# Sixteen-head attention on one core: q and k projected once per sequence and masked per quad of heads, the values' product between the two score passes of a turn

## The reference, cut to what matters

```
q = (src @ Wq + bq).reshape(B, T, 16, 8)      # k and v likewise
scores = einsum("bqhd,bkhd->bhqk", q, k) * 8 ** -0.5
probs  = softmax(scores, axis=-1)
out    = einsum("bhqk,bkhd->bqhd", probs, v).reshape(B, T, 128)
return out @ Wo + bo
```

## Time and profile before

| | us |
|---|---|
| median of 3 runs | 2275.07 (2269.94 to 2275.17) |
| profiled execution, span | 2277.2 |
| attention16, from its first matmul (163.7) to the next stage (504) | about 340 |
| busy in 163.7 to 504: PE, DVE, ACT | 332.69, 235.62, 195.37 |
| first scores (m = 0) at 169.03: 8 records at a granted clock of 0.50 | 2.08 |
| scores of m = 5, the first with turned scores, at | 180.7 |
| opening: GpSimd's last memset (L128) ends, next stage's first DVE instruction | 10.06, 13.40 |

### The profile page before, as it was taken

The page is one execution under the profiler, slowest core; times in us unless marked ns, Lnnn a source line. Parts: engine busy times, 40 slices in busy tenths (PEclk is TensorE's granted clock), DMA queues, the critical chain, the costliest instruction groups (busy, mean ns, idle before and its releaser), DMA issues. The chain is left out here.

```text
span 2277.2 us, 47255 instructions
## 1 busy us (share of the span) xinstructions
PE 2059.6 (90%) x18551; PEld 1392.9 (61%) x18551; DVE 1348.3 (59%) x3481; ACT 1049.2 (46%) x2520; POOL 631.5 (28%) x720
## 2 busy tenths in 40 slices
PE   4989999988879999698867897959999999999998
PEld 2546666657766677454555555655666666666565
DVE  2017777754555555456536884147877777677677
ACT  4235656642244454322234436345666666666222
POOL 3016930002210000103762015652333333333000
PEclk9989999998999999899986558988999999999999
DMA  2026030002110000241251013330000000000000
GB/s 62 19 29 29 2 39 2 2 5 65 18 55 1 1 1 1 69 140 22 39 138 39 2 28 114 48 87 25 1 1 1 1 1 1 1 1 1 6 15 19
DMA packets 118330, 64.44 MB, mean 28 GB/s; under 512 B 65848, under 2 KB 113248, under 8 KB 116960
## 3 DMA queue, kind: packets, MB, share of 16 engines
q1 hardware_dynamic: 106128, 52.37, 9.8%
q0 software_dynamic: 11264, 8.66, 2.7%
q10 hardware_dynamic: 720, 0.40, 0.1%
HBM read 37.54 MB, written 23.86 MB: 27 GB/s over the span
## 5 line engine op out<-in xcount | busy, mean ns | idle before, releaser
L3078 ACT ACTIVATE l_prob<-l_ps,l_neg_max 128x128 f32<-128x128 f32 (+1 forms) x512 | 208.6, 420 | 47.3 <-DVE l_neg_max L3177 42.5
L1658 ACT ACTIVATE l0a_prob<-l0a_pst 128x1024 f32<-128x1024 f32 x128 | 131.2, 1025 | 119.7 <-PE l0a_pst L1576 119.7
L2963 POOL TENSOR_TENSOR l_prob<-l_prob,l_total 128x256 f32<-128x256 f32 x128 | 78.6, 614 | 366.0 <-DVE l_total L3185 366.0
L1709 DVE TENSOR_REDUCE l0a_peak<-l0a_ps 128x4 f32<-128x1024 f32 x128 | 156.2, 1221 | 15.8 <-PE l0a_ps L1571 13.7
L1571 PE MATMUL l0a_ps<-l0a_k,l0a_q 32*128 32x256 f32 x1024 | 146.3, 405 | 3.3 <-ACT l0a_prob L1658 2.5
L680 ACT ACTIVATE l0e_hidden<-l0e_ph,l0f_b 128x512 f32<-128x512 f32 x128 | 87.9, 687 | 129.2 <-PE l0e_ph L591 129.2
L1576 PE MATMUL l0a_pst<-l0a_q,l0a_k 32*128 32x256 f32 x1024 | 145.8, 400 | 0.2 <-ACT l0a_prob L1658 0.2
L3173 DVE TENSOR_TENSOR l_ps<-l_ps,future 128x512 f32<-128x512 f32 x128 | 89.4, 699 | 93.2 <-PE l_ps L3009 93.0
L601 PEld LDWEIGHTS l0e_py<-l0f_w,l0e_hidden 128*128 128x128 f32 x1024 | 119.7, 192 | 35.0 <-ACT l0e_hidden L680 32.6
L2964 POOL TENSOR_TENSOR l_prob<-l_prob,l_total 128x512 f32<-128x512 f32 x128 | 133.2, 1041 | 0.0
L601 PE MATMUL l0e_py<-l0f_w,l0e_hidden 128*128 128x128 f32 x1024 | 129.8, 280 | 0.3 <-ACT l0e_hidden L680 0.3
(11 more groups left out here) (533 smaller groups left out, 4936.4 us busy)
## 6 DMA issues: line engine op xcount, KB each, us to landing
l_band<-zero SPq DMA_DIRECT2D x16, 272.0 KB, 7.3
x_tok<-in_x_dram SPq DMA_DIRECT2D x2, 2048.0 KB, 8.3
l2f_w<-in_L_ffn_w_dram SPq DMA_DIRECT2D x2, 2048.0 KB, 10.0
l_rows<-l_band SPq DMA_DIRECT2D x16, 256.0 KB
l1f_w<-in_L_ffn_W_dram SPq DMA_DIRECT2D x3, 1024.0 KB, 11.3
gd_tri<-gp_tri SPq DMA_DIRECT2D x8, 256.0 KB, 2.0
l0f_w<-gd_tri SPq DMA_DIRECT2D x8, 256.0 KB, 11.5
gd_tri<-l0f_w SPq DMA_DIRECT2D x8, 256.0 KB, 8.4
```

The lines of the kernel that those rows point to most:

```text
L1658: act.activation(prob[:, (n // 2) % 2, pair, :, :].rearrange("p g t s -> p g (t s)"), pst[:, :, :, :].rearrange("p g t s -> p g (t s)"), A ...
L1709: dve.tensor_reduce(to, ps[m % 2][:, :, :, :], AX.X, ALU.max, negate=True).then_inc(max_ready, 1)
L3078: act.activation(prob[:, m % 4, h, cols], ps[m % 2][:, h, cols], ACT.Exp, bias=neg_max[:, m % 4, h, t:t + 1], accum_out=total[:, m % 4, h, ...
```

## The change

`qk` is called once per sequence instead of once per quad: the weights are packed 128 x 128, and its result (q and k of all 16 heads) is copied by ACT from PSUM to a scratch buffer `raw` in SBUF (`save_raw`). Each quad's q and k are then made from `raw`: ACT multiplies q by a 0/1 column per partition and adds a masked bias (`mask_q`), DVE does the same for k (`mask_k`); rows that belong to other quads become 0 in q and 1 in k. A quad is now the heads s, 4+s, 8+s and 12+s. The maxima's tile `peak` is four-fold instead of two-fold. In `jobs(m)`, `pv` moves from odd to even steps, and `back`, `turn`, `qk`, `v`, `flip` and `out` all stand on odd steps, in this order. DVE's odd step is `normalize`, `highest`, `mask_k`, `add_peak`, `add_out`; its even step is `highest` alone. The `opening` builds the 0/1 columns on GpSimd and no longer clears the spaced weights.

```diff
@@ opening @@
-            pool.memset(h.wq[:, :, :], 0.0).then_inc(clear, 1)
-            pool.memset(h.wk[:, :, :], 0.0).then_inc(clear, 1)
-            pool.memset(h.bq[:, :], 0.0).then_inc(clear, 1)
-            pool.memset(h.bk[:, :], 1.0).then_inc(clear, 1)
...
+            pool.memset(h.eighth[:, :, :], 1.0).then_inc(clear, 1)
+            pool.wait_ge(clear, 3)
+            pool.affine_select(out=h.eighth[:, :, :], in_=h.eighth[:, :, :], compare_op=ALU.is_ge, fill=0.0,
+                               base=0, pattern=[[-32, 4], [-8, 4]], channel_multiplier=1).then_inc(cut, 1)
...
@@ jobs @@
-        if m % 2 == 1:
-            if 0 <= (m - 7) // 2 < ALL:
-                found.append(("pv", (m - 7) // 2))
+        if m % 2 == 0:
+            if 0 <= (m - 8) // 2 < ALL:
+                found.append(("pv", (m - 8) // 2))
+        else:
+            if 0 <= (m - 9) // 2 < ALL:
+                found.append(("back", (m - 9) // 2))
             if 0 <= (m - 3) // 2 < ALL:
                 found.append(("turn", (m - 3) // 2))
-        else:
-            if 0 <= (m - 8) // 2 < ALL:
-                found.append(("back", (m - 8) // 2))
-            if m // 2 + 2 < ALL:
-                found.append(("qk", m // 2 + 2))
             b = m // 8
-            if m % 8 == 4 and b < BATCH:
+            if m % 8 == 7 and b + 2 < BATCH:
+                found.append(("qk", b + 2))
+            if m % 8 == 5 and b < BATCH:
                 found.append(("v", b))
-            if m % 8 == 0 and 0 <= b - 2 < BATCH:
+            if m % 8 == 1 and 0 <= b - 2 < BATCH:
                 found.append(("flip", b - 2))
-            if m % 8 == 2 and 0 <= b - 2 < BATCH:
+            if m % 8 == 3 and 0 <= b - 2 < BATCH:
                 found.append(("out", b - 2))
         return found
+
+    def mask_at(m):
+        return (m + 3) // 2 if m % 2 == 1 and 2 <= (m + 3) // 2 < ALL else None
...
@@ PE @@
+                def qk(b):
+                    if x_turn["qk", b]:
+                        pe.wait_ge(px_free, x_turn["qk", b])
                     x = st.xnt[:, b * SEQ:(b + 1) * SEQ]
-                    pe.matmul(px[:, 0, :], wq[:, 4 * s:4 * s + 4, :], x, start=True, stop=True)
-                    pe.matmul(px[:, 1, :], wk[:, 4 * s:4 * s + 4, :], x, start=True, stop=True).then_inc(px_ready, 1)
+                    pe.matmul(px[:, 0, :], wq[:, :], x, start=True, stop=True)
+                    pe.matmul(px[:, 1, :], wk[:, :], x, start=True, stop=True).then_inc(px_ready, 1)
...
@@ ACT @@
+                def save_raw(b):
+                    act.wait_ge(px_ready, x_turn["qk", b] + 1)
+                    if b >= 2:
+                        act.wait_ge(k_saved, QUADS * (b - 1))
+                    act.activation(raw[:, b % 2, :, :], px[:, :, :], ACT.Copy).then_inc(px_free, 1)
+
+                def mask_q(n):
+                    act.wait_ge(shift_set, 3)
+                    act.wait_ge(px_free, x_turn["qk", n // QUADS] + 1)
                     if n >= 2 * QUADS:
                         act.wait_ge(turned_scores_ready, 2 * (n - 2 * QUADS) + 2)
                     s = n % QUADS
-                    act.activation(q[:, (n // QUADS) % 2, s, :], px[:, 0, :], ACT.Identity, bias=bq[:, s:s + 1]).then_inc(q_saved, 1)
+                    act.activation(q[:, (n // QUADS) % 2, s, :], raw[:, (n // QUADS) % 2, 0, :], ACT.Identity, bias=shift_q[:, s:s + 1],
+                                   scale=own[:, s:s + 1]).then_inc(q_saved, 1)
...
@@ DVE @@
-                    dve.tensor_scalar(k[:, (n // QUADS) % 2, s, :], px[:, 1, :], bk[:, s:s + 1], None, ALU.add).then_inc(px_free, 1)
+                    dve.tensor_scalar(k[:, (n // QUADS) % 2, s, :], raw[:, (n // QUADS) % 2, 1, :], own[:, s:s + 1], shift_k[:, s:s + 1],
+                                      ALU.mult, ALU.add).then_inc(k_saved, 1)
...
                 for m in range(STEPS):
-                    if m % 2 == 0:
-                        for what, n in jobs(m):
-                            if what == "back":
-                                normalize(n)
-                    else:
-                        for what, n in jobs(m - 1):
-                            if what == "qk":
-                                save_k(n)
+                    for what, n in jobs(m):
+                        if what == "back":
+                            normalize(n)
                     if m < PAIRS:
                         highest(m)
+                    if mask_at(m) is not None:
+                        mask_k(mask_at(m))
```

More of the change, by code:

```diff
@@ L1327, in __init__ @@
         heads, hd, row = 16, 8, 32
-        quads = heads // 4
-        self.wq = mem.sb("l0a_wq", [P, heads, row])
-        self.wk = mem.sb("l0a_wk", [P, heads, row])
+        self.wq = mem.sb("l0a_wq", [P, D])
+        self.wk = mem.sb("l0a_wk", [P, D])
         self.wv = mem.sb("l0a_wv", [P, D])
         self.wo = mem.sb("l0a_wo", [P, D])
-        self.bq = mem.sb("l0a_bq", [P, quads])
-        self.bk = mem.sb("l0a_bk", [P, quads])
+        self.bq = mem.sb("l0a_bq", [P, 1])
+        self.bk = mem.sb("l0a_bk", [P, 1])
         self.bv = mem.sb("l0a_bv", [P, 1])
         self.bo = mem.sb("l0a_bo", [P, D])
+        self.eighth = mem.sb("l0a_eighth", [P, 4, 4])
+        self.own = mem.sb("l0a_own", [P, 4])
         self.v = mem.sb("l0a_v", [P, 2, 2, heads, row])
-        self.peak = mem.sb("l0a_peak", [P, 2, 2, 4, row])
+        self.peak = mem.sb("l0a_peak", [P, 4, 2, 4, row])
     def pairs(self, a):
-        hd, row = 8, 32
-        found = [(self.wq[:, :, 0:hd], a["L0_ffn_Wq"]), (self.wk[:, :, 0:hd], a["L0_ffn_Wk"]),
+        row = 32
+        found = [(self.wq[:, :], a["L0_ffn_Wq"].rearrange("p h d -> p (h d)")), (self.wk[:, :], a["L0_ffn_Wk"].rearrange("p h d -> p (h d)")),
                  (self.wv[:, :], a["L0_ffn_Wv"].rearrange("p h d -> p (h d)")), (self.bo[:, :], a["L0_ffn_bo"])]
         for s in range(4):
[L1345 to L1348, removed]
+            mine = slice(row * s, row * s + row)
+            found += [(self.wo[mine, :], a["L0_ffn_Wo"].rearrange("g d s c -> s (g d) c")[s])]
+            for to, name in ((self.bq, "bq"), (self.bk, "bk"), (self.bv, "bv")):
+                found.append((to[mine, 0:1], a["L0_ffn_" + name].rearrange("g d s -> (g d) s")[:, s:s + 1]))
         return found
@@ L1451, in attention16 @@
     LAG = 5
-    STEPS = 8 * BATCH + 11
+    STEPS = 8 * BATCH + 12
     def heads_of(m):
@@ L1485, in attention16 @@
         mem = Memory(nc, ctx)
-        wq, wk, wv, wo, bq, bk, bv, bo, v, peak = h.wq, h.wk, h.wv, h.wo, h.bq, h.bk, h.bv, h.bo, h.v, h.peak
+        wq, wk, wv, wo, bq, bk, bv, bo, own, v, peak = h.wq, h.wk, h.wv, h.wo, h.bq, h.bk, h.bv, h.bo, h.own, h.v, h.peak
         q = mem.sb("l0a_q", [P, 2, QUADS, SEQ])
         k = mem.sb("l0a_k", [P, 2, QUADS, SEQ])
+        raw = spare.rearrange("p n x -> p (n x)")[:, 0:4 * SEQ].rearrange("p (b n x) -> p b n x", b=2, n=2)
+        shift_q = mem.sb("l0a_shift_q", [P, QUADS])
+        shift_k = mem.sb("l0a_shift_k", [P, QUADS])
         prob = mem.sb("l0a_prob", [P, 2, 4, 2, SEQ])
@@ L1672, in save_flip @@
                     act.activation(zt[:, :], pz[:, 0, :], ACT.Identity, bias=bv[:, 0:1]).then_inc(pz_free, 1)
-                save_q(0)
-                save_q(1)
+                save_raw(0)
+                mask_q(0)
+                mask_q(1)
+                save_raw(1)
                 for m in range(STEPS):
@@ L1678, in _ @@
                         exp(m - LAG)
+                    if mask_at(m) is not None:
+                        mask_q(mask_at(m))
                     for what, n in jobs(m):
                         if what == "qk":
-                            save_q(n)
+                            save_raw(n)
                         if what == "pv":
@@ L1692, in _, with set_shifts, mask_k @@
                 link = Chain(dve, recip_ready)
-                def save_k(n):
-                    dve.wait_ge(q_saved, n + 1)
+                def set_shifts():
+                    dve.tensor_scalar(shift_q[:, :], own[:, :], bq[:, 0:1], None, ALU.mult).then_inc(shift_set, 1)
+                    dve.tensor_scalar(shift_k[:, :], own[:, :], bk[:, 0:1], 1.0, ALU.mult, ALU.add).then_inc(shift_set, 1)
+                    dve.wait_ge(shift_set, 2)
+                    dve.tensor_tensor(shift_k[:, :], shift_k[:, :], own[:, :], ALU.subtract).then_inc(shift_set, 1)
+                    dve.wait_ge(shift_set, 3)
+                def mask_k(n):
+                    dve.wait_ge(px_free, x_turn["qk", n // QUADS] + 1)
                     if n >= 2 * QUADS:
```

46 lines of the change are left out of this document (25 added, 21 removed).

## The result

The change makes the kernel slower: 2334.42 us (median of 4 runs, 2328.70 to 2341.37) against 2272.51 (2266.82 to 2275.17) beside it, a ratio of 1.0272 [1.0246, 1.0298]. A later repetition gave 2345.41 against 2275.47 (1.0297 [1.0270, 1.0324]). 2314 was forecast, with a range of 2298 to 2342. The profiled execution took 2328.7 us, the shortest of the four; its span is 2327.1.

The account below looks back on a forecast made before the run. The prediction took the ring of scores, exponential and signal (2.40 us) as the bound: -15.8 + 9.8 + 1.8 + 35 + 10 - 3 + 1.3 = +39.1 us on the median 2275.07 gave 2314 us, range 2298 to 2342.

Parts of the forecast that it names:

- the wait of `qk`: PE at m % 8 = 7: qk waits for DVE's add_peak, 14 times, each step 2.5 us longer, 35 us.
- the ring of scores, exponential and signal: Attention steps on PE and ACT: scores, exponential and signal take 2.40 us per step, leaving 15.8 us at best to gain.
- S: The start of a step's scores on PE; qk was forecast to start at S + 3.81 us.
- fixed chain: The 127 attention steps without clock falls or waiting masks: ring, out and v, and 14 qk waits.
- The side estimate: DVE's mask_k at the skill page's doubled SBUF rate, fixed part unchanged: about 0.3 us, the sum 0.7 us less.
- The clock: PE's clock falls behind 7 of 14 qk waits, costing 1.4 to 1.5 us each, so 10 us.
- (b): Falls of PE's clock behind the qk waits, a part named after the result; forecast at 10 us.
- Rival 1: PE's clock stays at 1.00 behind every wait: +29, 2304 us; chance 0.27.
- rival 2: PE's clock falls behind all 14 qk waits and stays down long: +71, 2346 us; chance 0.14.
- Start: First attention steps: no qk stands in steps 0 to 4, so turned scores come earlier, -3 us.
- (c): DVE's mask_k waiting behind GpSimd's work, a part named after the result; the forecast had no such term.
- Rival 3: PE at m % 8 = 7: qk's wait is short, sum -2, 2273 us, not slower; chance 0.04.

Follow-up runs that it names:

- e6: Changed kernel with the jobs in the order of before, qk behind back at m % 8 = 6, and k's mask on ACT: 2273.71 us, ratio 0.9980 to before.
- e3: Changed kernel with DVE's add_peak moved ahead of highest and mask_k: 2297.33 us, ratio 1.0107 to before.
- e7: Changed kernel, its job order kept, with add_peak ahead of highest on DVE and k's mask on ACT: 2284.55 us, ratio 1.0044 to before.
- e1: Changed kernel with GpSimd's inversion of the gate matrices left out: 2337.67 us, one run.
- e2: Changed kernel with k's mask moved from DVE to ACT, one step earlier: 2323.06 us, ratio 1.0108 to before.
- a2: Changed kernel run again without any edit, beside a later set of runs: 2345.41 us.
- e9: Changed kernel with k's mask on ACT and four unread matmuls on PE ahead of each qk: 2293.45 us, ratio 1.0082 to before.

## Why the prediction was right, and where it was not

The direction and the main mechanism were right: the change is slower, and most of it is the wait of `qk` that was forecast. The size was low. The medians differ by 62 us where 39 were forecast; of the parts below, those that were measured in the stage add up to 56.

- The bound was read rightly. Steps without a further wait take 2.41 us; what bound them was the ring of scores, exponential and signal, and not PE's work. The 41 us of projections brought next to nothing (2.4 us, e6).
- `flip`, `out` and `v` take 2.44, 2.71 and 2.71 us, forecast 2.43, 2.71 and 2.71. In before the same steps, with a `qk` in them, took 2.53, 2.75 and 2.75, so here the change moved little. Behind `out` a step takes 2.47, which makes 1 us where 1.8 stood.
- The wait of `qk` was right. Its step takes 4.92 against 4.87, and `qk` starts at S + 3.86 against 3.81. `mask_k` undisturbed is 0.404, between the bounds, and makes the 0.05. The cause, DVE's order, is shown by e3 and e7, where the step is 3.46. In all the fixed chain came to 352.5 us, 351.4 by the forecast's terms.
- The side estimate, with the rate doubled and the fixed part unchanged, said "about 0.3" for `mask_k`. Its working gives more: by rows 6 the reduce of 1024 elements takes 1.22 us and `save_k` of 256 takes 0.47, hence some 0.25 for 256 elements, an estimate; half of that off 0.47 is 0.35. The sum hardly moves by it.
- The clock: the mechanism was right and so was the price of a fall (1.35 us in e1 against 1.45), but 7 falls of 14 were too few. Shown are 9 (after and e1), 11 (e2) and 12 (a2), and (b) is 12.7 us (e1) or 14.1 (e2) where 10 stood; e9 gives them back. Rival 1, no fall, did not come, and neither did rival 2, all 14 and 42 us.
- The term that failed is `mask_k`: "I take 0.35", with bounds of 0.29 and 0.47. Both rows come from stretches in which GpSimd stood still, and so does the window of the earlier trace rows. No term was given for GpSimd's work in the stage; the prediction looked at its opening alone, though before's stretch has 109.30 us of it. In after `mask_k` is up to 6.16 us under this work, and that costs 14.3 us (e1 against after). The nearest rows held the duration of the operation, and not what else reaches the same memory. This is the largest miss.
- Start: the first turned scores stand 13.07 us behind the first `qk` (16.98 before), -3.9 where -3 was forecast. Tail: from the last scores to the next stage's first matmul it is 9.09 instead of 7.78 us, +1.3 as forecast. In a2, the same program, this tail is 12.9, so it does not repeat either.
- The sum for the stage is -3.9 + 31.9 + 12.7 + 14.3 + 1.3 = +56.3 us, against +39.1. It closes because (b) and (c) are differences; the independent test is e9, which has neither: 346.2 us against a fixed chain of 347.0.
- The span grew by 49.9 us and the medians by 61.9. Of the 6.4 us by which the rest of the program is shorter in the profile of after, no run gives the cause, but a2 shows that such a difference comes by itself: behind the stage the same program takes 1762.6 us in one profile and 1770.4 in the other. And the profiled execution of after was the fastest of four, 5.7 us under their median.
- That the time fell into the range of 2298 to 2342 is in part luck. Its upper half was there for more and longer falls of the clock; most of the way from 2314 to 2334 us is the GpSimd term, which the forecast did not have.
- Rival 3, a short wait of `qk`, did not come; e6 shows what it would have needed, another order of the jobs.
